# A new written order for the attention chunks and the shared groups, and the routed groups' targets read on ScalarE's queue

## The chip, the cores and the metric

One core of one Trainium2 chip runs the whole program: TensorE (PE, with its weight loads as PEld), VectorE (DVE), ScalarE (ACT), GpSimd (POOL), SyncE (SP, which here only issues DMAs), and 16 DMA engines. The metric is the device time of one execution in microseconds. The kernel before has a median of 1469.2 us over 3 runs (1464.93 to 1469.47).

## The reference, cut to what matters

Two layers act on x of 4 x 1024 tokens by 256 features. Each adds a gated attention and a gated feed-forward part to x. The change lies in the first layer: 16-head attention of the tokens to 64 context keys, and a mixture of 16 experts with 4 per token beside one shared expert.

```python
x = x + tanh(g_xattn[0]) * L0_xattn(layernorm(x), ctx)       # 16 heads, 64 keys
x = x + tanh(g_ffn[0]) * L0_ffn(layernorm(x))
# L0_ffn, per token:
scores = sigmoid(xt @ gate_w.T); _, idx = top_k(scores + gate_b, 4)
w = take_along_axis(scores, idx); w = 2.5 * w / sum(w)
y = sum over the 4 chosen e of w[e] * (silu(gate_e(xt)) * up_e(xt)) @ w2_e.T
y = y + (silu(gate_s(xt)) * up_s(xt)) @ w2_s.T               # shared expert
# then the second layer: attention over context and tokens, a ternary-weight product
```

## The kernel before, in words

Each engine has one instruction stream, written by hand in the order in which it runs; semaphores join them. A wait on an engine holds everything behind it on that engine.

**Attention chunks.** The 4096 tokens are 8 chunks c of 512 (four tiles j of 128 tokens). For chunk c the streams do: layer norm statistics on DVE (`statistics(1, c)`, L834 to L844: bn_stats, bn_aggr, minus the mean into `nmu` at L843, variance into `ve` at L844); the power -0.5 and a product on POOL (`rstd_of`, L644 and L646); four normalisations on ACT (`normalised`, L721) into the one tile `xn`; transposes on PE into the banks x0, x1 (L1085), moved to SBUF by ACT (all moves are L726); the query products q0, q1 (L1096), moved too; per tile the scores (L1106 a mask term, L1109), the row maximum and the shift on DVE (`shift`, L860 and L862), exp on ACT (L736), the row sum and its reciprocal on DVE (`row_sum`, L868 and L871), the scaling on POOL (`normalise`, L652); eight pairs of transposes pt0 to pt7 (L1118); values oT0, oT1 (L1128); outputs o0, o1 (L1138); and DVE's addition to x (`add`, L877).

The routing of chunk c runs one chunk later, among the attention of c + 1: `statistics(2, c)`, `rstd_of`, `normalised` (L721 again), the high half of the row in fp16 on ACT (`rows_high`, L753) and the low half on DVE (`rows_low`, L883), transposes r0, r1, logits (L1148), tanh (L761), `choose` on DVE (L888 to L921), `targets` (L926 to L931), `ranks` on PE (L1157 to L1162), `slots` (L939 to L948, which reads the rank bank at L939), and 16 `send`s on POOL (L659), indirect DMAs that scatter the rows to per-expert lists in HBM (`expert_rows`). The dense rows go to HBM by SP (`store_dense`). Beside each chunk ACT and DVE also split the weights of two experts into high and low fp16 halves (`high`, L713 and L714; `low`, L849 and L851).

All PSUM products of this part go round a ring of four banks in the fixed order of the list `order`: product i may be written only when product i - 4 has been read by the engine that the list names for it ("act" or "dve").

**Groups.** When the last chunk is out of the ring, the shared expert runs over 16 groups of 256 tokens, then the routed experts over 79 groups of 256 rows. For group g SP issues a DMA transpose of the rows (`shared_rows`, L599; routed L624) into one of 4 buffers; PE does gate and up (`group_gate_up`, L1218, 12 matmuls); ACT silu (L810); DVE the product with up (L1028); ACT the high half (L815); DVE the low half (L1033); PE the down product (`group_down`, L1229, 6 matmuls); DVE adds a shared result to x (L1039) or copies a routed one to one of 6 buffers (`group_out`, L1047). PE is two groups ahead with gate and up (DEEP = 3). Before the routed groups can start, 16 tails of the lists have to be filled with spare rows (`fill_tail`, L557, 272 KB each; 5 by ACT, 11 by SP between its shared transposes), for which the counts of all chunks must be known (`tables`, L960 gives the first table, L976 the second), and all sends and fills must have landed.

For a routed group SP also reads the targets of its 256 rows (L630, 1 KB into `gidx`, 8 buffers, in SP's queue behind the group's transpose), and POOL scatters the result with two indirect DMAs (L703), which wait for `gidx` and for the copy; the copy waits until the scatter six groups before has landed (`s_back`). SP's reads wait for the landing eight groups before. The next stage starts when the last scatter has landed.

## Time and profile before

| what | value |
|---|---|
| median of 3 runs | 1469.2 us |
| the profiled execution | 1465.75 us, span 1464.0 us |
| busy: PE, DVE, ACT, POOL | 77%, 69%, 45%, 34% of the span |
| mean granted TensorE clock | 0.884 |
| attention chunks and routing | to about 389 us |
| shared groups and tails | to about 434 us |
| routed groups | to 670 us |

Times in the rows are in us from the start of the span. A busy share is a mean over stages with different limits, so the stage is read first (the windows), then the engine that is busy in it, and then what ends that engine's waits (the bracket at the end of a timeline's row: idle time before it, and who ended it).

### The profile page before, as it was taken

What the parts mean: (1) busy time and instruction counts of PE and PEld (TensorE: products, weight loads), DVE (VectorE), ACT (ScalarE), POOL (GpSimd) and SP (SyncE); (2) the same over time, 40 slices, a digit from 0 to 9 for tenths busy, and PEclk for the clock granted to TensorE, in tenths of its full rate; (3) what the DMA queues carried; (4) which work ended last, traced back from release to release, by engine and by line L of the source; (5) the groups of instructions that cost most, each with busy time, mean ns of one, the idle gap of its engine ahead of it and who ended that gap; (6) DMA issues with size and microseconds to landing.
All of it is one profiled execution on the core that took longest, in us unless ns stands there. A gap on an engine that the chain in (4) does not pass through costs nothing. (4 is left out here: it accounts for less than half of the span.)

```text
span 1464.0 us, 25236 instructions
## 1 busy us (share of the span) xinstructions
PE 1126.2 (77%) x8327; PEld 606.6 (41%) x8327; DVE 1007.6 (69%) x1863; ACT 664.6 (45%) x1401; POOL 503.9 (34%) x576
## 2 busy tenths in 40 slices
PE   3786777775487777781877589999999999988858
PEld 2343344434375666660444123333333333331646
DVE  3677887875564544444996778888888888860665
ACT  1454344453232322220333066777776777775430
POOL 1226655666716766673000611112111111111110
PEclk7898879877699999995889589999999999995989
DMA  6011222222888888874796411211112111100003
GB/s 194 22 36 59 73 93 82 86 94 75 235 198 170 172 167 181 172 154 183 228 286 213 132 41 49 68 41 40 40 41 62 56 40 40 41 2 0 1 1 115
DMA packets 203515, 145.81 MB, mean 100 GB/s; under 512 B 134392, under 2 KB 178427, under 8 KB 203402
## 3 DMA queue, kind: packets, MB, share of 16 engines
q1 hardware_dynamic: 180778, 102.76, 28.1%
q0 software_dynamic: 13728, 34.64, 7.0%
q10 hardware_dynamic: 8896, 6.90, 1.6%
q8 instruction: 71, 1.16, 0.3%
q14 instruction: 42, 0.34, 0.1%
HBM read 53.19 MB, written 69.75 MB: 84 GB/s over the span
## 5 line engine op out<-in xcount | busy, mean ns | idle before, releaser
L1788 DVE TENSOR_REDUCE small<-ps 128x2 f32<-128x960 f32 (+6 forms) x384 | 379.0, 1041 | 56.7 <-PE ps L1843 56.5
L1767 ACT ACTIVATE region<-ps 128x512 f32<-128x512 f32 (+5 forms) x768 | 343.1, 533 | 107.9 <-PE ps L1857 106.5
L1738 POOL TENSOR_SCALAR_AFFINE_SELECT region<-region 128x512 f32<-128x512 f32 (+2 forms) x160 | 87.3, 546 | 425.7 <-ACT region L1767 425.7
L1857 PE MATMUL ps<-region 50*128 50x512 f16 (+5 forms) x896 | 197.7, 330 | 27.2 <-ACT region L1767 23.9
L1933 PE MATMUL ps<-region 128*32 128x512 f32 (+5 forms) x1792 | 191.6, 501 | 2.5 <-POOL region L1738 1.9
L703 POOL DMA_INDIRECT result_rows<-region,small x158 | 157.9, 999 | 99.2 <-DVE region L1047 58.4
L1218 PE MATMUL ps<-region 128*128 128x256 f16 x1140 | 149.8, 285 | 53.8 <-DMA region<-expert_rows 45.8
L1843 PE MATMUL ps<-region 48*128 48x480 f16 (+6 forms) x896 | 141.6, 334 | 13.5 <-DVE small L1788 11.3
L1218 PEld LDWEIGHTS ps<-region 128*128 (+1 forms) x1140 | 110.0, 102 | 88.9 <-issue 67.5
L1857 PEld LDWEIGHTS ps<-region 50*128 50x128 f16 (+1 forms) x896 | 54.4, 95 | 209.7 <-ACT region L1767 195.1
L1028 DVE SCALAR_TENSOR_TENSOR region<-ps,region 128x256 f32<-128x256 f32 x95 | 40.3, 424 | 128.9 <-ACT region L810 123.6
L652 POOL TENSOR_TENSOR region<-region,small 128x1024 f32<-128x1024 f32 x32 | 61.5, 1933 | 111.0 <-DVE small L871 110.9
L810 ACT ACTIVATE region<-ps 128x256 f32<-128x256 f32 x95 | 36.3, 383 | 133.6 <-PE ps L1218 129.3
L1229 PE MATMUL ps<-region 128*128 (+1 forms) x570 | 81.2, 281 | 9.0 <-DVE region L1033 9.0
L1838 PE MATMUL ps<-small 64*128 64x128 bf16 (+1 forms) x768 | 68.7, 245 | 16.7 <-POOL small L1719 11.6
L726 ACT ACTIVATE small<-ps 128x512 f32<-128x512 f32 x64 | 36.2, 590 | 88.8 <-PE ps L1096 53.4
L659 POOL DMA_INDIRECT expert_rows<-region,small x64 | 65.4, 1022 | 28.0 <-issue 17.1
L1529 PE MATMUL ps<-region 128*128 128x512 f16 (+1 forms) x240 | 56.1, 402 | 23.7 <-DVE region L1472 23.7
L659 POOL DMA_INDIRECT expert_rows<-rows_odd,small x64 | 64.7, 1012 | 23.2 <-issue 19.3
L1843 PEld LDWEIGHTS ps<-region 48*128 48x128 f16 x896 | 49.1, 97 | 51.3 <-DVE small L1788 47.2
L721 ACT ACTIVATE xn<-x_sb,small,rstd 128x256 f32<-128x256 f32 x64 | 33.1, 589 | 82.0 <-POOL small L646 82.0
L1096 PE MATMUL ps<-small 128*128 128x512 f32 x64 | 47.9, 918 | 27.2 <-DVE x_sb L877 19.3
(219 smaller groups left out, 1735.3 us busy)
## 6 DMA issues: line engine op xcount, KB each, us to landing
region<-result_rows SPq DMA_DIRECT2D x16, 1024.0 KB, 6.8
region<-v_parts SPq DMA_DIRECT2D x16, 576.0 KB, 4.0
v_parts<-region SPq DMA_DIRECT2D x14, 576.0 KB, 6.9
region<-k_parts SPq DMA_DIRECT2D x96, 68.0 KB, 2.2
region<-q_parts SPq DMA_DIRECT2D x96, 64.0 KB, 2.1
k_parts<-region SPq DMA_DIRECT2D x16, 272.0 KB, 4.4
x_sb<-in_x ACTq DMA_DIRECT2D x8, 512.0 KB, 9.0
region<-in_w13T SPq DMA_DIRECT2D x16, 256.0 KB, 3.2
```

Source lines behind the costliest of these rows:

```text
L652: nc.gpsimd.tensor_tensor(pr, pr, rsum[:, j, :].unsqueeze(2).to_broadcast([P, H, CTX]), ALU.mult).then_inc(s_prob, 1)
L659: nc.gpsimd.indirect_dma_start(out=xs, out_offset=bass.IndirectOffsetOnAxis(ap=sloti[:, b, at_:at_ + 1], axis=0), in_=rows[b][:, at_ // TO ...
L703: nc.gpsimd.indirect_dma_start(out=ys, out_offset=bass.IndirectOffsetOnAxis(ap=gidx[:, r % I_BUFS, j:j + 1], axis=0), in_=y_out[:, r % Y_B ...
L1218: ins = nc.tensor.matmul(ps[:, 2 * (g % DEEP) + half_, 0:GROUP], w, xgT[:, g % G_BUFS, part, kh, :], start=n == 0, stop=n == 5)
L1229: ins = nc.tensor.matmul(ps[:, 6 + g % 2, j * D:(j + 1) * D], (hgh, hgl)[part][:, g % DEEP, j * P:(j + 1) * P], flat((w2h, w2l)[low][:, ba ...
L1738: nc.gpsimd.affine_select(out=t, in_=t, compare_op=ALU.is_ge, fill=0.0, base=r0, pattern=[[0, G], [1, w]], channel_multiplier=-1).then_inc ...
L1767: nc.scalar.activation(dst, src, ACT.Exp, scale=SCALE).then_inc(s_exp, 1)
L1788: nc.vector.tensor_reduce(nmp[:, qt, :, p0:p0 + np_, place], s_pair(n + first)[:, :, 0:np_ * nk] .rearrange("p e (h k) -> p e h k", h=np_) ...
L1838: nc.tensor.matmul(o, mask_id[rows[half], part, :], mask_dg[rows[half], part, 0:np_, :], start=part == 0, stop=False, skip_group_check=True)
L1843: ins = nc.tensor.matmul(banks[half][:, p * nk:(p + 1) * nk], q_of(r, v)[:, p0 + p, qt * P:(qt + 1) * P], k_of(r, v)[:, p0 + p, k0:k0 + nk ...
L1857: ins = nc.tensor.matmul(o, k_of(rr, tbuf)[:, pair, kt * P:kt * P + rows], q_of(rr, tbuf)[:, pair, q0:q0 + nq], start=True, stop=True)
L1933: ins = nc.tensor.matmul(ps[32 * h:32 * h + 32, O_BANK, q0 - hf * CH:q0 - hf * CH + nq], vg[0:rows, buf, (kt * G + h) * 32:(kt * G + h + 1 ...
```

## The change

It has four parts.

1. The written order of the attention chunks. The transposes and moves of x (`inputs`) become ring entries of their own, done for chunk c + 2 at the end of chunk c. ACT does the experts' high halves ahead of the query moves. DVE does `statistics(1, c + 2)` right behind `statistics(2, c - 1)`, and `add(c)` ahead of row sums 2 and 3. PE does `ranks(c - 1)` behind the last scores. POOL sends 4 rows of the newest chunk late in a chunk and the other 12 at the front of the next.
2. Two sets of `nmu`, `nmr`, variance and rstd in place of one, so that waits on them look one event further back.
3. The first shared groups are written among the routing of the last chunk. Gate and up of a group share one bank, shared results have one bank (`DEEP`), so the groups need only four banks while the ring still runs. ACT fills 8 tails among groups 6 to 13, SP the other 8.
4. The reads of the routed groups' targets go from SP's queue to ACT's (`load_targets`), three groups ahead, between a group's silu and its high half. Each now loads the group's start from the table again.

```diff
-            order = queries(0)
+            order = inputs(0) + queries(0) + inputs(1)
             for c in range(CHUNKS):
-                order += queries(c + 1) if c < LAST else []
+                order += queries(c + 1)
                 order += probs_of(c, range(2)) + rows_of(c - 1) + probs_of(c, range(2, 4)) + logits_of(c - 1)
-                order += probs_of(c, range(4, 8)) + ranks_of(c - 1) + outputs_of(c)
+                order += probs_of(c, range(4, 8)) + values_of(c)
+                if c < LAST:
+                    order += ranks_of(c - 1) + inputs(c + 2) + outputs_of(c)
+                else:
+                    order += outputs_of(c) + ranks_of(c - 1)
...
+            def load_targets(eng, r):
+                if r >= I_BUFS:
+                    old = r - I_BUFS
+                    eng.wait_ge(s_back[old % Y_BUFS], (old // Y_BUFS + 1) * GT * 16)
+                first = start(eng, FIRSTS + r)
+                eng.dma_start(gidx[:, r % I_BUFS, :],
+                              xs[bass.ds(first, GROUP), bass.ds(first >> SHIFT, 1)].bitcast(I32)
+                              .rearrange("(j p) n -> p (j n)", p=P),
+                              allow_slow_non_contiguous=True).then_inc(s_idx[r % I_BUFS], 16)
...
@@ POOL, chunk c; EARLY, LATE = 4, 6 @@
                     if c >= 2:
-                        send(c - 2, 8, 16)
+                        send(c - 2, EARLY, LATE)
+                    if c + 2 < CHUNKS:
+                        rstd_of(1, c + 2)
+                    if c >= 2:
+                        send(c - 2, LATE, 16)
                     if c < LAST:
                         normalise(c + 1, range(2))
-                    if c and c < LAST:
-                        send(c - 1, 0, 2)
-                    if c + 2 < CHUNKS:
-                        rstd_of(1, c + 2)
-                    if c and c < LAST:
-                        send(c - 1, 2, 8)
-                    if c < LAST:
+                        if c:
+                            send(c - 1, 0, EARLY)
                         normalise(c + 1, range(2, TC))
...
@@ ACT, chunk c @@
+                    for expert in experts_beside(c):
+                        high(*expert)
                     if c < LAST:
                         move_queries(c + 1)
                     if c:
                         normalised(2, c - 1)
-                    for expert in experts_beside(c):
-                        high(*expert)
...
                     silu(g)
+                    if FIRSTS <= g < ALL_GROUPS - AHEAD:
+                        load_targets(act, g - FIRSTS + AHEAD)
+                    hidden_high(g)
...
@@ DVE, chunk c @@
+                        second(c - 1)
+                    if c + 2 < CHUNKS:
+                        statistics(1, c + 2)
                     for expert in experts_beside(c):
                         low(*expert)
...
-                    if c + 2 < CHUNKS:
-                        statistics(1, c + 2)
-                    if more:
-                        shift(c + 1, 3)
-                        row_sum(c + 1, 2)
-                        row_sum(c + 1, 3)
+                    shift(c + 1, 3)
                     add(c)
+                    row_sum(c + 1, 2)
+                    row_sum(c + 1, 3)
...
@@ PE, chunk c @@
-                    if c:
-                        ranks(c - 1)
                     values(c)
                     if more:
                         scores(c + 1, 3)
+                        if c:
+                            ranks(c - 1)
+                    if c + 2 < CHUNKS:
+                        inputs_of(c + 2)
                     outputs(c)
...
@@ PE, after the chunks @@
+                group_step(0)
+                transposed(LAST, 2, ("r0", "r1"))
+                group_step(1)
+                logits(LAST)
+                group_step(2)
+                ranks(LAST)
```

## Rows read from the trace of the kernel before

**Rows 1.** Busy by stage: us, PE, PEld, DVE, ACT, POOL (instructions), PEclk, DMA share, GB/s.
```profile
223.39:265.10 41.71, 29.01 (x138) 17.43 (x136) 33.75 (x74) 19.09 (x36) 26.25 (x24) 0.88 0.25 85
341.20:370.10 28.90, 19.14 (x91) 14.37 (x91) 11.42 (x40) 11.38 (x22) 18.23 (x20) 0.65 0.33 98
389.20:429.50 40.30, 28.88 (x228) 23.25 (x225) 24.14 (x50) 11.84 (x28) 15.80 (x16) 0.84 0.99 245
442.20:669.80 227.60, 168.14 (x1373) 132.16 (x1370) 106.97 (x232) 62.55 (x154) 157.91 (x158) 0.94 0.81 162
```

**Rows 2.** DVE's timeline in one chunk: start, us, instruction, count [idle before <- releaser].
```profile
245.55 2.15 DVE L943 TENSOR_TENSOR small<-small 128x256 f32<-128x256 f32 x1
...
255.40 1.22 DVE L868 TENSOR_REDUCE small<-region 128x16 f32<-128x1024 f32 x1 [2.67 <-ACT region L736]
...
261.40 2.19 DVE L843 TENSOR_SCALAR small<-mv 128x4 f32<-128x4 f32 x1
...
268.03 0.69 DVE L849 SCALAR_TENSOR_TENSOR region<-region 128x512 f16<-128x512 f32 x1 [4.37 <-ACT region L714]
```

**Rows 3.** ACT's timeline in the same chunk, the normalisation of layer 1.
```profile
252.35 2.08 ACT L721 ACTIVATE xn<-x_sb,small,rstd 128x256 f32<-128x256 f32 x4 [9.57 <-POOL small L646]
```

**Rows 4.** PE's timeline in the same chunk.
```profile
253.09 2.71 PE L1085 MATMUL ps<-ident,xn 128*128 128x128 f32 x8 [5.28 <-ACT xn L721]
258.90 5.33 PE L1096 MATMUL ps<-small 128*128 128x512 f32 x8 [3.10 <-DVE x_sb L877]
...
267.10 1.04 PE L1085 MATMUL ps<-ident,xn 128*128 128x128 f32 x8
```

**Rows 5.** POOL's timeline in the same chunk, and before the last.
```profile
245.51 1.90 POOL L652 TENSOR_TENSOR region<-region,small 128x1024 f32<-128x1024 f32 x1 [7.84 <-DVE small L871]
...
259.79 3.76 POOL L652 TENSOR_TENSOR region<-region,small 128x1024 f32<-128x1024 f32 x2
263.74 1.04 POOL L644 TENSOR_TENSOR rstd<-ve,half 128x4 f32<-128x4 f32 x1 [0.19 <-DVE ve L844]
...
270.79 0.96 POOL L659 DMA_INDIRECT expert_rows<-rows_odd,small  x1 [0.30 <-issue]
...
342.95 3.76 POOL L652 TENSOR_TENSOR region<-region,small 128x1024 f32<-128x1024 f32 x2
```

**Rows 6.** SP's routed transposes and target reads by source: ns min/median/max, first and last start.
```profile
L624 SPq DMA_TRANSPOSE region<-expert_rows x79: 1234/1257/2087, 429.6 to 652.2; - x79
...
L630 SPq DMA_DIRECT2D small<-expert_rows x79: 381/386/1676, 431.1 to 653.7; - x79
```

**Rows 7.** POOL's scatters of results by source.
```profile
L703 POOL DMA_INDIRECT result_rows<-region,small x158: 982/985/2137, 442.2 to 667.7; - x158
```

**Rows 8.** Waits between engines, 442 to 670 us: total us, times, longest us.
```profile
POOL result_rows L703 <- DVE region L1047: 58.4, 33, 30.6
```

**Rows 9.** Busy while PE's first transposes of the chunk run (columns of rows 1).
```profile
253.10:255.80 2.70, 2.67 (x8) 1.43 (x8) 0.40 (x1) 2.70 (x5) 2.09 (x3) 0.50 0.32 103
```

**Rows 10.** DVE's timeline: ends of statistics (chunks 0, 5, 6), last addition, first table.
```profile
92.97 0.16 DVE L844 TENSOR_SCALAR ve<-mv 128x4 f32<-128x4 f32 x1
...
305.23 0.16 DVE L844 TENSOR_SCALAR ve<-mv 128x4 f32<-128x4 f32 x1
...
341.15 0.16 DVE L844 TENSOR_SCALAR ve<-mv 128x4 f32<-128x4 f32 x1
...
369.36 0.75 DVE L877 SCALAR_TENSOR_TENSOR x_sb<-ps,tg,x_sb 128x512 f32<-128x512 f32 x1 [0.97 <-PE ps L1138]
...
388.88 0.28 DVE L960 TENSOR_TENSOR small<-ps,small 1x16 int32<-1x16 f32 x1
```

**Rows 11.** ACT's queue: its five tail fills, in one stretch.
```profile
390.18 8.20 ACTq L557 DMA_DIRECT2D expert_rows<-region  x5
```

**Rows 12.** ACT's loads of a table word for the fills, by source: ns min/median/max.
```profile
L556 ACTq TENSOR_LOAD <-small x5: 467/690/1132, 389.3 to 396.3; - x5
```

**Rows 13.** The sends to the lists, from issue to landing, 180 to 420 us.
```profile
DMA to landing us min/median/max: 2.4/2.5/6.0
```

More of the change, by code:

```diff
@@ L405, in flamingo @@
         junk = view(small, "junk", [P, 4], F32)
-        nmu = view(small, "nmu", [P, TC], F32)
-        nmr = view(small, "nmr", [P, TC], F32)
+        nmu = view(small, "nmu", [P, 2, TC], F32)
+        nmr = view(small, "nmr", [P, 2, TC], F32)
+        vars_ = view(small, "vars", [P, 2, TC], F32)
+        rstds = view(small, "rstds", [P, 2, TC], F32)
         gw_sb = view(small, "gw", [P, KH, E], F32)
@@ L1053, in _, with group_step @@
-                for g in range(ALL_GROUPS):
+                    shift(c + 1, 3)
+                    add(c)
+                    row_sum(c + 1, 2)
+                    row_sum(c + 1, 3)
+                add(LAST)
+                second(LAST)
+                targets(LAST - 1)
+                slots(LAST - 1)
+                def group_step(g):
                     if g + DEEP - 1 < ALL_GROUPS:
@@ L1061, in _ @@
                         group_hidden_low(g + DEEP - 1)
+                for g in range(DEEP - 1):
+                    group_hidden(g)
+                    group_hidden_low(g)
+                rows_low(LAST)
+                group_step(0)
+                group_step(1)
+                choose(LAST)
+                targets(LAST)
+                slots(LAST)
+                tables()
+                for g in range(2, ALL_GROUPS):
+                    group_step(g)
                     if g == SPLIT_AT:
@@ new lines, in group_down @@
+                def group_down(g, e):
+                    eng.wait_ge(s_ghl, g + 1)
+                    if 0 < g < FIRSTS:
+                        eng.wait_ge(s_yout, g)
+                    elif g >= FIRSTS + 2:
+                        eng.wait_ge(s_yout, g - 1)
+                    elif g >= FIRSTS:
+                        eng.wait_ge(s_act, moved(turn[LAST, "lg"]))
+                        eng.wait_ge(s_dve, moved(turn[LAST, "count"]))
+                    for j in range(GT):
+                        for n, (part, low) in enumerate(three):
+                            ins = nc.tensor.matmul(result(g)[:, j * D:(j + 1) * D],
+                                                   (hgh, hgl)[part][:, g % DEEP, j * P:(j + 1) * P],
+                                                   flat((w2h, w2l)[low][:, bass.ds(e, 1), :]), start=n == 0, stop=n == 2)
+                    ins.then_inc(s_gy, 1)
@@ L1165, in _, with expert, inputs_of @@
+                def expert(g):
+                    return start(eng, g) >> SHIFT if g >= FIRSTS else E
+                def inputs_of(c):
+                    transposed(c, 1, ("x0", "x1"))
+                inputs_of(0)
                 queries_of(0)
                 wait_moved(0, "q1")
-                for j in range(TC):
-                    scores(0, j)
+                scores(0, 0)
+                scores(0, 1)
+                inputs_of(1)
+                scores(0, 2)
+                scores(0, 3)
@@ L1223, in group_down @@
-                def group_down(g, e):
-                    eng.wait_ge(s_ghl, g + 1)
-                    if g >= 2:
-                        eng.wait_ge(s_yout, g - 1)
-                    for j in range(GT):
-                        for n, (part, low) in enumerate(three):
-                            ins = nc.tensor.matmul(ps[:, 6 + g % 2, j * D:(j + 1) * D],
-                                                   (hgh, hgl)[part][:, g % DEEP, j * P:(j + 1) * P],
-                                                   flat((w2h, w2l)[low][:, bass.ds(e, 1), :]), start=n == 0, stop=n == 2)
-                    ins.then_inc(s_gy, 1)
@@ L1234, in expert, with group_step @@
-                def expert(g):
-                    return start(eng, g) >> SHIFT if g >= FIRSTS else E
-                experts = []
-                for g in range(DEEP - 1):
-                    experts.append(expert(g))
-                    group_gate_up(g, experts[-1])
-                for g in range(ALL_GROUPS):
+                ranks(LAST - 1)
+                def group_step(g):
                     if g + DEEP - 1 < ALL_GROUPS:
@@ L1247, in _ @@
                     group_down(g, experts.pop(0))
+                experts = []
+                for g in range(DEEP - 1):
+                    experts.append(expert(g))
+                    group_gate_up(g, experts[-1])
+                group_step(0)
+                transposed(LAST, 2, ("r0", "r1"))
+                group_step(1)
+                logits(LAST)
+                group_step(2)
+                ranks(LAST)
+                wait_free(LAST, "count")
+                nc.tensor.matmul(slot(LAST, "count")[:, 0:E], onesb[:], counts[:, CHUNKS, :], start=True,
+                                 stop=True).then_inc(s_full, 1)
+                for g in range(3, ALL_GROUPS):
+                    group_step(g)
         reset(region1, region2, small)
```

222 lines of the change are left out of this document (116 added, 106 removed).

## The prediction

> **What bounds the kernel now.** I read the table by stages first [rows 1]. The change touches the first 670 us, and four stretches of it behave differently. In the attention chunks (the first row is one chunk of about 42 us) DVE is busy 33.75 of 41.71 us and no DMA or PE share is near full. Round the last chunk, 341 to 370 us, every engine is idle a third of the time or more. From 389 to 430 us the 16 DMA engines are busy 0.99. In the routed groups (442 to 670) the DMA share is 0.81 and POOL, whose 157.9 us of issues leave out the 0.30 us between two of them, is the fullest engine.
>
> Second view, the timelines of one chunk. DVE's instructions follow each other without a gap but for two waits [rows 2]: 2.67 us before the third row sum (for ScalarE's exp) and 4.37 us before the low halves of the experts' weights (for ScalarE's high halves). ScalarE is late for both because of what stands ahead in its queue: it sat 9.57 us for POOL's rstd of chunk c+2, whose statistics DVE makes late in the chunk [rows 3], and the high halves (L713, L714) stand behind the query moves, which wait for PE, which waited 3.10 us for DVE's addition [rows 4]. So add, queries, query moves, normalise, high halves, low halves, scores is a loop round four engines, and it closes once a chunk. Two DVE instructions are long only because POOL's multiplication L652 runs beside them [rows 2, 5]: L943 takes 2.15 us and ends when L652 does, L843 takes 2.19 and ends when L652 does.
>
> Third, the routed groups. SP issues 79 transposes from 429.6 to 652.2, 222.6/78 = 2.854 us apart, and between two of them stands one read of targets of 0.39 us [rows 6]. POOL's 158 scatters start from 442.2 to 667.7 [rows 7], and of the 58.4 us that it stood for DVE's results 30.6 lie before the first [rows 8]: 27.8 us inside the stage.
>
> **The change part by part.**
>
> *Attention order.* The x transposes of chunk c+2 now run at the end of chunk c, so the queries no longer wait for the addition; the bank of q0 and q1 is freed by ScalarE's x moves. High halves go ahead of the query moves: 4.37 us gone. statistics(1, c+2) moves to the front of the chunk, POOL's rstd right behind it, ScalarE has it some 10 us before it needs it: 2.67 gone. The two sets of nmu, rstd and nmr let both rstd stand at once and cost no instruction. Left on DVE, with the small gaps between its instructions: 41.71 - 4.37 - 2.67 = 34.67 us. The addition now stands before row sums 2 and 3, so POOL's two L652 end only some 0.6 us after DVE reaches L843, where they now hold it 2.0: 34.67 - 1.5 = 33.2.
>
> What is late next: POOL. Its queue per chunk is 16 sends of 0.96 + 0.30, four L652 of 1.9 and two rstd of about 1.4, together 20.2 + 7.6 + 2.8 = 30.6 us; the sends 4 to 16 of c-2 now fill the 7.84 us in which it waited for a row sum [rows 5]. Walking through one chunk, POOL's last L652 ends 0.1 us before DVE's statistics end, so the two are level. PE has its queries done early and then waits some 4 us for that last L652. In the trace 5.28 us of waiting were followed by a granted clock of 0.50 (1.2 GHz) [rows 9]; its 8 transposes then took 2.71 us, and 1.04 in the dense stretch at 267 [rows 4]. I charge the first scores at half clock to DVE: 1.3 us. Chunk: 34.5 us. Ends: 30.9 (no L652 in DVE's way: 34.67 - 2.0 - 1.7) and 39.2 (POOL's 31.4 with hiccups plus the 7.84 us wait unfilled).
>
> From the end of the statistics of chunk 0 to those of chunk 5 the trace has 305.23 - 92.97 = 212.3 us [rows 10]; five of 34.5 are 172.5: -39.8. Chunk 6, which has no further chunk to prepare, 341.15 - 305.23 = 35.9, becomes 34.5 - 2.1 (no statistics) = 32.4: -3.5. In the start the low halves wait no longer for the query moves, but inputs(1) come ahead of scores: -2 (0 to -4). Sum -45.3.
>
> *Last chunk.* Now POOL's rstd of chunk 6 stands behind two L652 that end at 346.7 [rows 5], 5.4 us after the statistics (341.3), and from there to the end of the last addition (370.1 [rows 10]) it is 23.4 us. Afterwards those L652 are done when the statistics are, and the same chain starts 5.4 us earlier: -5.4.
>
> *Shared groups beside the last routing.* DVE reaches the tail table (L960) 18.8 us after the last addition [rows 10]. In the new order statistics (2.2), targets and slots of chunk 6 (2.5), two shared groups of hidden halves (2.8), the wait for ScalarE's normalise and rows_high (3.1), rows_low and two group steps (5), and choose to slots (8, partly a wait for the logits) stand ahead: 24 to 25 us, so +6. After it come 16 tail fills, 16 sends and the transposes: 40.3 us at 0.99 busy [rows 1], so DMA and not compute is the limit. Two transposes have gone ahead; a routed group's whole DMA is 0.81 x 227.6/79 = 2.3 us [rows 1], its transpose the larger part, so I take 3.3 us for two, and the gate comes some 37 us after the tail table. The hidden shared groups therefore buy little. Sum +2; ends -12 (fills overlapping better, tail table no later) and +10 (tail table 6 later, three more ScalarE table loads, and ScalarE's eight fills, about 1.64 us each by the five that took 8.20 [rows 11], standing ahead of silu).
>
> *Targets on ScalarE.* SP loses 0.39 + 0.27 us a group and then paces at about 2.1. POOL's two scatters are 2 x (0.99 + 0.30) = 2.58 us [rows 5, 7] and become the pace. ScalarE gains a load of a start-table word (0.47 to 1.13 us in its fills, while DMA was full [rows 12]), register work of some 0.4, and the issue of 0.39: 1.3 to 1.5 us between silu (0.38) and the high half (0.42), about 2.2 us a group, under 2.58. DEEP groups in flight hide the longer path: a group's hidden half is wanted two groups later. From 2.87 a group (225.5/78.5 [rows 7]) to 2.68 (POOL's 2.58, hiccups, late landings): 79 x 0.19 = -15. Ends: -22 (all at 2.6) and +5.
>
> The Trainium skill ("DMA: Bandwidth & Descriptors", section "Issuing engines are not separate DMA queues") says that DMAs of all issuing engines share the same 16 engines and that issuing from several saves only the sequencer's time. By it SP's 0.66 us x 79 = 52 us is the most that the move can free, and none of it if the 16 engines set the pace. The trace has them at 0.81, or 184 us of 227.6; that is rival 1.
>
> **Sum**, against the profiled execution's 1465.75 us (span 1464.0): -45.3 - 5.4 + 2 - 15 = -63.7, so 1402. The median of the runs, 1469.2, is 3.4 above that execution; I give 1403.
>
> **Rivals.**
> 1. *The routed stage gains nothing*: the DMA engines, or ScalarE waiting for landings, hold it at 2.87. For: mean share 0.81 hides stretches at full. Against: POOL stood 27.8 us for DVE only, and 184 us is under 204. Time 1403 + 15 = 1418.
> 2. *POOL paces the attention* at 39.2: five chunks x 4.7 = +23.5, 1426. For: 30.6 of 33.2 us leaves little room for a long send. Against: its waits are at the places that the sends now fill. With rival 1: 1441.
> 3. *The new order does nothing for DVE*: PE's outputs(c) now wait for slots(c-1) through the bank ring (o1 after rank), and what DVE won it waits for the addition. Then only the queue move counts, 1450; with rival 1 about 1465. Against: slots read the rank 5 us before the addition is due and PE's second half of outputs takes 1.8.
> 4. *Slower*: ScalarE's read for group r+3 waits for the landing of scatter r-5, and high halves of r and silu of r+1 queue behind it, DVE behind those. The loop over four groups is 1.29 + landing + 4.3 us (read 1.4, high half and silu 0.9, hidden 0.5, result 0.7, POOL's 0.8). With landings of 2.5, the nearest row's median, it gives 2.0 us a group, with its maximum of 6.0 [rows 13] 2.9. To eat the 48.7 us of the other terms the pace must be 2.87 + 0.62 = 3.49, landings of 8.4 us on the mean; at 9.5 the pace is 3.77 and the time 1403 + 86 = 1489.
>
> **How the numbers follow.** Forecast 0.52 (its own range 1388 to 1417), rival 1 0.19, rival 2 0.12, both 0.06, rival 3 0.06, of which 0.02 near 1465, rival 4 0.05. Range 1384 (chunk 33.2 and routed -21, with -5 at the tail) to 1440, which leaves out rivals 3 and 4 and some of the fastest. About 0.3% (4.4 us) is what a measurement here can tell from no change: faster 0.93, same 0.02, slower 0.05.
>
> **What would show it.** Right: DVE's waits for L713/L714's results and for the third exp gone; statistics(2, c) 33 to 36 us apart; L843 under 1 us; the first routed transpose near 380; POOL's scatters 2.6 to 2.75 apart with hardly a wait for the result copies. Wrong: POOL without an idle stretch and chunks at 38 or more; PE waiting before L1138's second bank; the tail fills ending before 370; ScalarE idle before its high half for a DMA of result rows; transposes landing later than the groups need them.

## The result, and the profile after

The changed kernel takes 1411.07 us (median of 4 runs, 1404.78 to 1412.54) against 1468.1 us for the kernel before (4 runs): a ratio of 0.9606, 95% interval 0.9573 to 0.9640. Its profiled execution takes 1411.37 us (span 1409.6). The forecast was 1403, with 1384 to 1440 around it.

The stages first, as in [rows 1]. Each chunk runs from one `statistics(2, c)` to the next; the last four stretches run to the last addition, to the tail table, to the first routed transpose, and from the first routed result to the last scatter. The gate is what the first routed transpose waits for: all sends to the lists and all tail fills must have landed.

```profile
core 0: us, PE busy (x) PEld busy (x) DVE busy (x) ACT busy (x) POOL busy (x), PEclk, DMA share, GB/s
90.53:125.01 34.48, 27.35 (x134) 16.44 (x134) 32.57 (x75) 18.84 (x34) 14.84 (x12) 0.91 0.17 56
125.01:161.25 36.24, 29.10 (x134) 18.06 (x134) 33.90 (x76) 18.96 (x34) 26.28 (x24) 0.88 0.29 98
161.25:198.10 36.85, 29.75 (x134) 18.06 (x134) 33.85 (x75) 18.95 (x34) 26.89 (x24) 0.87 0.27 97
198.10:231.63 33.53, 27.08 (x134) 16.63 (x134) 31.88 (x76) 18.83 (x34) 26.81 (x24) 0.91 0.31 106
231.63:265.48 33.85, 27.38 (x134) 16.77 (x134) 31.90 (x75) 18.84 (x34) 27.12 (x24) 0.90 0.30 105
265.48:301.46 35.98, 23.14 (x118) 14.68 (x118) 31.96 (x65) 15.17 (x26) 25.96 (x22) 0.78 0.29 99
301.46:323.40 21.94, 19.10 (x90) 14.50 (x90) 8.87 (x31) 11.03 (x19) 13.85 (x16) 0.64 0.46 119
323.40:345.45 22.05, 15.65 (x120) 12.03 (x120) 16.23 (x60) 7.48 (x17) 14.87 (x15) 0.92 0.75 213
345.45:388.51 43.06, 24.75 (x165) 18.45 (x166) 21.25 (x44) 7.56 (x20) 19.60 (x20) 0.72 0.95 230
400.02:611.77 211.75, 170.10 (x1380) 129.27 (x1380) 109.17 (x235) 56.78 (x155) 157.67 (x158) 0.96 0.88 173
```

The chunk of 41.7 us in [rows 1] has become 33.5 to 36.9 us with DVE busy 31.9 to 33.9 of it. The routed stretch has lost 15 us at the same POOL time, and its DMA share has risen from 0.81 to 0.88.

DVE in chunk 5, then in chunk 6 (start, duration, engine, line, operation; the bracket is the idle time ahead):

```profile
236.26 1.22 DVE L911 TENSOR_REDUCE small<-ps 128x16 f32<-128x1024 f32 x1 [0.77 <-PE ps L1171]
240.15 1.23 DVE L911 TENSOR_REDUCE small<-ps 128x16 f32<-128x1024 f32 x1 [0.28 <-PE ps L1171]
249.47 0.22 DVE L982 SCALAR_TENSOR_TENSOR region<-small 128x64 int32<-128x64 f32 x1
253.61 2.15 DVE L994 TENSOR_TENSOR small<-small 128x256 f32<-128x256 f32 x1
264.61 0.80 DVE L894 TENSOR_SCALAR small<-mv 128x4 f32<-128x4 f32 x1
...
270.25 1.23 DVE L911 TENSOR_REDUCE small<-ps 128x16 f32<-128x1024 f32 x1 [2.90 <-PE ps L1171]
283.46 2.21 DVE L982 SCALAR_TENSOR_TENSOR rows_odd<-small 128x64 int32<-128x64 f32 x1
289.59 2.15 DVE L994 TENSOR_TENSOR small<-small 128x256 f32<-128x256 f32 x1
```

Both waits of [rows 2], for the third exp and for the high halves, are gone; what is left are short waits for the scores. Three instructions are long, L894, L982 and L994, and POOL's queue shows why: each ends with one of its multiplications or up to 0.3 us after it.

```profile
253.58 1.90 POOL L675 TENSOR_TENSOR region<-region,small 128x1024 f32<-128x1024 f32 x1 [0.72 <-DVE small L922]
261.63 3.76 POOL L675 TENSOR_TENSOR region<-region,small 128x1024 f32<-128x1024 f32 x2
283.67 1.91 POOL L675 TENSOR_TENSOR region<-region,small 128x1024 f32<-128x1024 f32 x1
289.56 1.90 POOL L675 TENSOR_TENSOR region<-region,small 128x1024 f32<-128x1024 f32 x1 [3.98 <-DVE small L922]
```

In the routed groups POOL's waits for DVE (total, times, longest) can be held against [rows 8]: there 58.4 with 30.6 before the first scatter, 27.8 inside; here 12.0 inside, of which 23 of the 28 waits are the ordinary 0.30 us between two scatters. The scatters run from 401.6 to 611.8, 2.68 us a group. The third row, of what waited for their landing, is rival 4's wait: ScalarE stands 55.5 us in 17 places behind its read. It costs little, but not nothing: the five real waits of POOL, 0.73 to 1.27 us and 5.0 together, each follow one of these places. The last three rows are one of them, where ScalarE's 5.20 us (a DMA's landing, so the bracket names no engine) reach POOL as 0.86.

```profile
POOL result_rows L725 <- DVE region L1061: 40.8, 29, 28.8
...
L725 POOL DMA_INDIRECT result_rows<-region,small x158: 984/986/1781, 401.6 to 611.8; - x158
  ACT region L798: 55.5, 17
...
469.66 0.42 ACT L798 ACTIVATE region<-region 128x256 f16<-128x256 f32 x1 [5.20 <-issue]
470.11 0.43 DVE L1047 TENSOR_TENSOR region<-region 128x256 f16<-128x256 f32 x1 [4.53 <-ACT region L798]
472.30 0.98 POOL L725 DMA_INDIRECT result_rows<-region,small  x1 [0.86 <-DVE region L1061]
```

### The profile page after: what moved, and what is told of

The parts are those of the page before. It is cut to its first block and busy times, and to the rows that moved or that the text cites. A ratio compares the mean times of both kernels' runs of the same rounds, so it can differ in the third digit from the quotient of the medians.

```text
span 1409.6 us, 25476 instructions
## 1 busy us (share of the span) xinstructions
PE 1113.5 (79%) x8327; PEld 599.3 (43%) x8327; DVE 1006.2 (71%) x1863; ACT 657.6 (47%) x1401; POOL 509.4 (36%) x576
## 3 DMA queue, kind: packets, MB, share of 16 engines
q8 instruction: 71, 1.16, 0.3%
## 5 line engine op out<-in xcount | busy, mean ns | idle before, releaser
L1868 DVE TENSOR_REDUCE small<-ps 128x2 f32<-128x960 f32 (+6 forms) x384 | 378.9, 1040 | 56.8 <-PE ps L1923 56.5
L725 POOL DMA_INDIRECT result_rows<-region,small x158 | 158.6, 1004 | 81.3 <-DVE region L1061 40.8
L798 ACT ACTIVATE region<-region 128x256 f16<-128x256 f32 x95 | 39.6, 416 | 162.0 <-DVE region L1042 62.6
L1256 PE MATMUL ps<-region 128*128 (+1 forms) x570 | 81.6, 282 | 31.9 <-DVE region L1047 17.2
L1047 DVE TENSOR_TENSOR region<-region 128x256 f16<-128x256 f32 x95 | 40.2, 423 | 85.2 <-ACT region L798 83.5
L1180 PE MATMUL ps<-ident,region 128*128 128x128 f32 x256 | 43.9, 316 | 46.6 <-POOL region L675 45.0
L1256 PEld LDWEIGHTS ps<-region 128*128 128x128 f16 x570 | 55.0, 101 | 47.1 <-issue 37.6
L1171 PE MATMUL ps<-region,small 128*128 128x512 f32 x128 | 74.0, 663 | 0.0
L760 ACT ACTIVATE region<-region 128x1024 f32<-128x1024 f32 x32 | 33.9, 1058 | 81.6 <-DVE region L913 81.6
```

What stands on the lines that cost most here:

```text
L725: nc.gpsimd.indirect_dma_start(out=ys, out_offset=bass.IndirectOffsetOnAxis(ap=gidx[:, r % I_BUFS, j:j + 1], axis=0), in_=y_out[:, r % Y_B ...
L1171: ins = nc.tensor.matmul(o, qT[:, m, j * P:(j + 1) * P], kbd[:, m, c // 2, :], start=False, stop=True)
L1256: ins = nc.tensor.matmul(result(g)[:, j * D:(j + 1) * D], (hgh, hgl)[part][:, g % DEEP, j * P:(j + 1) * P], flat((w2h, w2l)[low][:, bass.d ...
L1868: nc.vector.tensor_reduce(nmp[:, qt, :, p0:p0 + np_, place], s_pair(n + first)[:, :, 0:np_ * nk] .rearrange("p e (h k) -> p e h k", h=np_) ...
```

## The experiments

Times are medians, beside runs of the kernel before on the same chip (1464.5 to 1467.1 us); the changed kernel itself (1411.1) was not run again beside them. Chunk times and waits are those of one profiled execution of each kernel.

**1. The order alone.** The reads go back behind SP's transposes.

```diff
                     sp.dma_start_transpose(... xs[bass.ds(first, GROUP), E:ROW] ...)
+                    read_targets(sp, g - FIRSTS, first)
...
-                        for r in range(AHEAD):
-                            load_targets(act, r)
...
-                    if FIRSTS <= g < ALL_GROUPS - AHEAD:
-                        load_targets(act, g - FIRSTS + AHEAD)
```

> The new order with the reads of the targets back on SP, one behind each transpose. Theory (SP's queue set the routed pace before, and the move alone changed it): the scatters fall back from 2.68 to 2.85-2.88 us a group, the first scatter to the last takes 225 us rather than 210, SP hardly waits for the gate products, the stages before the first routed transpose keep their times within 1 us, and the time is 1411 + 15 = 1426. Rival (the routed pace came with the new order: other banks, silu and high half split on ScalarE): 2.68 stays and the time is 1411.

1424.0 us, ratio 0.9712 (0.9677 to 0.9747); 2.855 us a group. One part of the theory fails: with the same code ahead of it, the first routed transpose stands 61.0 us behind the last addition and not 65.1. That stretch varies from one execution to the next, which matters for the tail below.

**2. The reads alone**, in the old order:

```diff
-                    sp.dma_start(gidx[:, r % I_BUFS, :], ...)
...
                     silu(g)
+                    if FIRSTS <= g < ALL_GROUPS - 3:
+                        load_targets(g - FIRSTS + 3)
+                    hidden_high(g)
```

> The old order with only the reads of the targets moved to ScalarE's queue, three groups ahead, between silu and the high half. Theory (the two parts of the change are independent and add): the routed pace goes from 2.87 to 2.68, every stage before it keeps its time, 1468 - 15 = 1453. Rival (the move needs the new order's free ScalarE or its banks): the pace stays at 2.8 or more and the time at 1463 to 1470.

1451.8 us, ratio 0.9897 (0.9875 to 0.9920); 2.69 us a group. The routed stretches of the two, from first result to last scatter:

```profile
395.45:621.07 225.62, 166.14 (x1380) 128.88 (x1380) 107.73 (x235) 62.98 (x155) 156.34 (x157) 0.98 0.81 164
```

```profile
440.13:652.90 212.77, 169.74 (x1380) 126.96 (x1377) 108.94 (x235) 56.34 (x155) 156.76 (x157) 0.97 0.85 172
```

42.1 us for the order and 14.4 for the reads are 56.5, and both together gave 57.0: within the intervals (some 5 and 3 us) the two parts add. Both rivals of experiments 1 and 2 fall, and rival 1 of the prediction with them.

**3. Statistics late.** `statistics(1, c + 2)` and its rstd on POOL go back to their old places, the rest of the new order stays. DVE's part:

```diff
-                    if c + 2 < CHUNKS:
-                        statistics(1, c + 2)
                     for expert in experts_beside(c):
                         low(*expert)
...
                         slots(c - 1)
+                    if c + 2 < CHUNKS:
+                        statistics(1, c + 2)
```

> The changed kernel with statistics(1, c+2) put back on DVE behind slots, and POOL's rstd of it behind the first two multiplications; the rest of the new order stays. Theory (ScalarE's wait for the rstd, 9.57 us in the old chunk, comes back and with it DVE's wait for the third exp, 2.67 us; and the 2.0 us of statistics no longer fill DVE's wait for the first scores): 2.7 + 1 to 2 us in five chunks, 1411 + 21 = 1432. Rival (the rstd is early enough in either place, because the inputs' transposes were moved to the end of the chunk): the chunks keep their times within 0.5 us, 1411 +- 3.

1458.4 us, ratio 0.9953 (0.9929 to 0.9976): 47 us worse than the changed kernel, twice the theory's 21. The old wait did not come back where it was. One chunk of 44.4 us:

```profile
206.40 2.15 DVE L994 TENSOR_TENSOR small<-small 128x256 f32<-128x256 f32 x1
219.88 0.75 DVE L928 SCALAR_TENSOR_TENSOR x_sb<-ps,tg,x_sb 128x512 f32<-128x512 f32 x1 [6.28 <-PE ps L1200]
213.45 2.98 PE L1148 MATMUL ps<-ident,xn 128*128 128x128 f32 x8 [12.38 <-ACT xn L743]
216.22 5.39 PE L1200 MATMUL ps<-small 128*128 128x256 f32 x16
212.70 2.08 ACT L743 ACTIVATE xn<-x_sb,small 128x256 f32<-128x256 f32 x4 [15.95 <-POOL small L669]
```

The inputs' transposes of c + 2 (L1148) now stand ahead of the outputs (L1200) on PE. With the rstd late ScalarE waits 15.95 us, PE 12.38, the outputs and DVE's addition 6.28. Without the early statistics the transposes of the inputs hold up everything behind them there.

**4. High halves behind.**

```diff
-                    for expert in experts_beside(c):
-                        high(*expert)
                     if c < LAST:
                         move_queries(c + 1)
                     if c:
                         normalised(2, c - 1)
+                    for expert in experts_beside(c):
+                        high(*expert)
```

> The changed kernel with ScalarE's high halves put back behind the query moves and the second norm; the rest of the new order stays. Theory (the queries no longer wait for the addition, but the second norm waits for POOL, which has its last multiplications ahead of it: ScalarE's high halves end 4 to 5 us later, DVE's low halves stand before the first shift and come 2.3 to 3.2 us late): 2.7 us in each of six chunks, 1411 + 16 = 1427. Rival 1 (the prediction's own price, the 4.37 us wait of the old chunk, returns whole): 1411 + 26 = 1437. Rival 2 (with the queries early, the place of the high halves is of no account): 1411.

1419.3 us, ratio 0.9689 (0.9645 to 0.9733). The middle chunks take 37.3 us. The theory's place is right, its price half: DVE waits 2.37 us for the high halves, but the scores are there when it is done, so the old wait of [0.77] for them goes.

```profile
204.06 0.69 DVE L900 SCALAR_TENSOR_TENSOR region<-region 128x512 f16<-128x512 f32 x1 [2.37 <-ACT region L736]
205.94 1.22 DVE L911 TENSOR_REDUCE small<-ps 128x16 f32<-128x1024 f32 x1
```

**5. Scores first.** On PE the first scores go ahead of the transposed probabilities, into the gap in which it waits for POOL.

```diff
-                    transposed_probs(c, range(2))
                     if more:
                         wait_moved(c + 1, "q1")
                         scores(c + 1, 0)
+                    transposed_probs(c, range(2))
```

> On PE the first scores of chunk c+1 ahead of the first two pairs of transposed probabilities of chunk c, and not behind them. PE then makes them while POOL still multiplies. Theory (DVE bounds the chunk, and its waits for the scores, 0.5 to 2.9 us for the first and 0.3 to 0.5 for the second, 9.5 us over six chunks, lie on the path): the waits go, the chunks take 33.4 us on the mean and not 35.0, 1411 - 9.5 = 1401.5. Rival (POOL's queue, sixteen sends of 1.27, four multiplications and two rstd, 31 of 34 us, bounds the chunk too): DVE waits for the transposed probabilities' followers instead, the chunks lose 0.3 us, 1409.

1398.9 us, ratio 0.9524 (0.9489 to 0.9559), a little more than the theory gave. Chunks 2 to 5 take 32.7 us each with DVE busy 31.8, chunk 1 35.0 and chunk 6 37.6. Chunks 4 and 5, where L982 was not held before, lose 0.9 and 1.2 us, about their old waits for the scores (0.75 and 1.05). Chunks 2 and 3 lose 3.6 and 4.2: their waits (1.44 and 2.10) and the 2.0 us of L982, which no longer meets a multiplication. In chunk 6 nothing is won: DVE waits 1.72 us for ScalarE and 3.16 for the second scores, and L961 is held 2.14 us.

```profile
221.60:254.30 32.70, 27.37 (x139) 16.36 (x138) 31.80 (x75) 18.74 (x34) 26.15 (x24) 0.99 0.31 109
254.30:291.90 37.60, 23.03 (x112) 14.55 (x113) 31.89 (x65) 15.06 (x26) 24.84 (x22) 0.76 0.28 95
```

**6. Slots late.** On DVE the writing instruction of targets and all of slots but the read of the rank bank go behind `shift(c + 1, 3)`, out of the way of POOL's second multiplication.

```diff
                     if c:
-                        slots(c - 1)
+                        place_of(c - 1)
                     shift(c + 1, 3)
+                    if c:
+                        slots(c - 1)
...
```

> On DVE the last of targets (L982) and all of slots but its read of the rank bank go behind shift(c+1, 3), where POOL's second multiplication has ended; the order on PE is that of the changed kernel. Theory (DVE instructions that read and write SBUF are held while POOL multiplies: L994 took 2.15 us beside L675 and 0.43 without, L982 2.2 and 0.22; but the chunk is closed by the scores behind POOL's last multiplication, so DVE wins the time and waits it out): L994 falls to 0.43 and L982 to 0.22, the chunks with the held L982 (36.2, 36.9, 36.0 us) come to some 34, the others lose 0.5 at most: 1411 - 8 = 1403. Rival 1 (DVE's queue alone bounds the chunk): 1.7 us in each of six chunks and 2.0 in three of them, 1411 - 16 = 1395. Rival 2 (POOL, whose four sends now start as late as before, bounds it): 1409 to 1412.

1400.4 us, ratio 0.9557 (0.9517 to 0.9597): all chunks at 34.2 to 35.0, none at 36. Chunks 2, 3 and 6, the ones with the held L982, lose 1.8 to 2.6 us, the others grow by 0.3 to 0.7. That is 4.7 us in all; the median's 10.6 are not the hold alone. In the profiled execution (1398.1) another 4.0 us lie between the last chunk and the last addition, in code that the edit does not touch and at a granted clock of 0.82 (the last row; the changed kernel took 21.94 us there at 0.64). The held instructions are short now (L992 is the old L982, L997 the old L994), but another one, L894, stands 3.12 us and ends with POOL's last pair of multiplications (224.76 + 3.76). A hold that is taken off one instruction fell on the next.

```profile
218.43 0.22 DVE L992 SCALAR_TENSOR_TENSOR rows_odd<-small 128x64 int32<-128x64 f32 x1
218.56 0.42 DVE L997 TENSOR_TENSOR small<-small 128x256 f32<-128x256 f32 x1
225.44 3.12 DVE L894 TENSOR_SCALAR small<-mv 128x4 f32<-128x4 f32 x1
224.76 3.76 POOL L675 TENSOR_TENSOR region<-region,small 128x1024 f32<-128x1024 f32 x2
...
296.96:314.95 17.99, 15.68 (x98) 11.78 (x99) 8.92 (x31) 10.69 (x19) 13.91 (x16) 0.82 0.58 129
```

**7. Scores first and slots late together.**

> The first scores ahead of the transposed probabilities (which took the time to 1398.9 and five chunks to 32.7 us, DVE busy 31.8 of them) and the slots behind shift(c+1, 3) together. Theory (with the scores ready in time DVE's queue is the bound, and the 1.7 us in which L994 is held by POOL's multiplication come off it whole until POOL's 31.0 us are reached): 31.1 us a chunk, 1398.9 - 1.6 x 6 = 1389. Rival (POOL is the bound at 32.7 already, since its last four sends start only when the slots are there): the chunks stay at 32.4 or more, 1397 to 1400.

1408.4 us, ratio 0.9626 (0.9561 to 0.9692), with single runs from 1402.5 to 1419.6: worse than experiment 5, and no better than 6. L894 is held 3.11 us, and chunks 2 to 4 take 34.1 to 34.7 as in experiment 6. Chunks 5 and 6 take 38.3 and 38.1. There POOL's first multiplication meets other instructions of `choose`, L966 (0.17 us alone) and L961 (0.42), and POOL then stands 5.56 and 6.57 us for the next row sum. So the theory falls, and the rival too: POOL is not the bound in these two chunks, which are 4 us slower than in experiment 6; the hold has moved once more.

```profile
244.59 2.57 DVE L966 TENSOR_TENSOR small<-small 128x16 bf16<-128x16 bf16 x1
281.69 2.78 DVE L961 TENSOR_TENSOR small<-small 128x256 f32<-128x256 f32 x1
...
252.69 1.90 POOL L675 TENSOR_TENSOR region<-region,small 128x1024 f32<-128x1024 f32 x1 [5.56 <-DVE small L922]
290.75 1.90 POOL L675 TENSOR_TENSOR region<-region,small 128x1024 f32<-128x1024 f32 x1 [6.57 <-DVE small L922]
```

**8. Fewer sends ahead of the last multiplications** (slots late kept).

```diff
-                EARLY, LATE = 4, 6
+                EARLY, LATE = 2, 4
```

> The late slots, and on POOL two sends of the newest rows ahead of the last two multiplications of a chunk and not four (EARLY 2, LATE 4); PE's order is that of the changed kernel. Theory (with the late slots alone the hold only changed its victim: L994 fell to 0.43 us, but POOL's last two multiplications then started 1.2 us after the row sums allow, and L894, which stood beside them, was held 3.12 us; two sends fewer, 2.5 us, let them start earlier): L894 near 0.9, 34.2 us a chunk become 32.3, where POOL's own 27.0 of work, 4.8 between sends and 0.3 beside them are the bound, 1400.4 - 6 x 1.9 = 1389. Rival (the sends taken from there stand ahead of the first two multiplications in the next chunk, which come 2.5 us later, and the probabilities' transposes with them): 34 us or more a chunk, 1398 to 1403.

1391.0 us, ratio 0.9476 (0.9441 to 0.9510), the fastest measured, and the theory's mechanism: L894 is at 0.80, and the five chunks take 32.9 us on the mean. From chunk 2 on POOL has no idle stretch but one of 1.4 to 1.7 us for the slots (and up to 0.3 between two instructions), while DVE waits 0.6 to 1.7 us for the first scores.

```profile
215.80 3.75 POOL L675 TENSOR_TENSOR region<-region,small 128x1024 f32<-128x1024 f32 x2 [0.26 <-DVE small L922]
```

```profile
218.78 0.80 DVE L894 TENSOR_SCALAR small<-mv 128x4 f32<-128x4 f32 x1
```

**9. Experiments 5, 6 and 8 together.**

> The first scores ahead of the transposed probabilities, the late slots, and EARLY 2, LATE 4. Theory (DVE then waits for no scores and is held by no multiplication but 0.9 us at L894, so that POOL's queue, some 32 us, is the bound): 32.0 us a chunk, against 32.7 with the scores alone, 1398.9 - 0.7 x 6 - 2 (chunk 6) = 1393. Rival (POOL without idle time closes the chunk through its last multiplications whatever DVE wins, as with scores and slots together, 34.2 to 38.3 us): 1400 or more.

1395.1 us, ratio 0.9527 (0.9502 to 0.9552). The five chunks take 33.1 us: on top of experiment 8 the scores' place is worth nothing. The theory's 1393 is 2 us off, but its premise does not hold: DVE now waits 1.2 to 3.3 us a chunk for the second scores. POOL waits up to 0.6 us for row sums in chunks 2 to 5, so it is the bound, or nearly.

**10. Tail fills denser.** ScalarE's eight fills two to a shared group.

```diff
-                    if TAILS_FROM <= g < TAILS_FROM + ACT_TAILS:
-                        fill_tail(act, g - TAILS_FROM)
+                    if TAILS_FROM <= g < TAILS_FROM + ACT_TAILS // 2:
+                        fill_tail(act, 2 * (g - TAILS_FROM))
+                        fill_tail(act, 2 * (g - TAILS_FROM) + 1)
```

> ScalarE's eight tail fills two to a shared group (groups 6 to 9) and not one to each of 6 to 13; nothing else. Theory (the gate before the routed groups is held by the last fill, which stands in ScalarE's queue behind the silu of shared group 12, and that waits for a late transpose; SP waited 5.61 us for it): the last fill is issued near 372 and not at 385.2, the first routed transpose leaves near 383 and not at 388.5, 1411 - 5.5 = 1405.5. Rival (the 16 DMA engines, 0.95 busy between the tail table and the gate, set it): the gate moves by less than 1 us, 1411. Second rival: two fills ahead of a silu hold shared groups 6 to 9 back by 1.6 us each, gate/up of group 12 is what SP then waits for, and the time is 1411 to 1416.

1411.7 us, ratio 0.9624 (0.9598 to 0.9650): no gain. ScalarE's last fill left at 367.9 and not at 385.2, but SP's transposes were then held in their issue, and its own last fill went out at 377.4. In SP's queue of this kernel, against the 1.23 us of a routed one:

```profile
364.13 5.64 SPq L628 DMA_TRANSPOSE region<-dense_rows  x1
371.25 5.33 SPq L628 DMA_TRANSPOSE region<-dense_rows  x1
384.80 1.23 SPq L655 DMA_TRANSPOSE region<-expert_rows  x1
```

The gate moved by 2.3 us against the tail table (40.8 and not 43.1 us behind it), and the first routed result came 4.5 us later behind it. The time is the rival's. That the DMA engines set the gate is not shown by it: in the runs that leave this stretch as it is, the gate stands 38.5 to 43.1 us behind the table, and 40.8 lies among them.

**11. Last routing ahead of all shared groups**, as before the change. DVE's part of the edit (ScalarE and PE likewise):

```diff
-                for g in range(DEEP - 1):
-                    group_hidden(g)
-                    group_hidden_low(g)
                 rows_low(LAST)
-                group_step(0)
-                group_step(1)
                 choose(LAST)
...
```

> The changed kernel with the last chunk's routing put back ahead of all shared groups on ScalarE, DVE and PE; the rest of the new order, the eight tail fills on ScalarE and the reads of the targets too, stays. Theory (shared groups between the steps of the last routing buy nothing, since the DMA engines are what the gate waits for, and they push the tail table back): the tail table comes 19 us after the last addition and not 22.05, the first routed transpose 59 to 60 us after it and not 60.9 to 65.1, and the time is 1411 - 3 = 1408. Rival (the shared groups that now run ahead are what lets the first routed group start 11.5 us behind its gate): the gate is 3 us earlier, the first result 3 to 8 us later, 1411 to 1416.

1413.1 us, ratio 0.9648 (0.9616 to 0.9680). The tail table comes at 18.9 us, as the theory says, but the gate only 49.1 behind it, 68.0 after the last addition and not 59 to 60. The theory falls, and so does the rival, whose gate was to be earlier. With the shared groups ahead the gate stands 60.7 to 65.1 us behind the last addition, so they do save something, 2.9 us or more in this one profile, which the medians hardly show.

**12. Chunk 6's sends ahead of the last additions**, on top of experiment 8. DVE's and POOL's parts (PE's ranks and the bank order follow):

```diff
+                targets(LAST - 1)
+                place_of(LAST - 1)
+                slots(LAST - 1)
                 add(LAST)
                 second(LAST)
-                targets(LAST - 1)
-                place_of(LAST - 1)
-                slots(LAST - 1)
...
+                send(LAST - 1, 0, 4)
                 rstd_of(2, LAST)
-                send(LAST - 1, 0, 16)
+                send(LAST - 1, 4, 16)
```

> The kernel with the late slots and EARLY 2, and in the last chunk the rank, targets and slots of chunk 6 ahead of the last additions (DVE waited 4.0 us there), with four of its sends ahead of the last rstd; everything else as in e10_slots_early2. Theory (the gate before the routed groups follows POOL's last sends: 32 of them, 41 us, are left at the last addition, and in the changed kernel none of chunk 6's can start before the last statistics, where the kernel before had its slots ready): chunk 6's sends start 6 to 8 us earlier, chunk 7's 16 start when their slots are there and not behind them, the last send leaves 4 us earlier against the last addition (44.5 and not 48.4 us after it), the first routed transpose 60.5 and not 65.1, and the time is 1391 - 4.5 = 1386.5. Rival (the 16 DMA engines, 0.95 busy from the tail table to the gate, set it, or the shared groups do): the last send moves and the gate does not, 1390 to 1392.

1391.9 us, ratio 0.9482 (0.9457 to 0.9506), no change from experiment 8. The last send left 42.6 us after the last addition and not 48.4, the first transpose 61.9 and not 65.1. SP then waited 6.7 us for landings where it had waited 4.6. The last send moved as the theory says. Whether the gate followed cannot be told: 61.9 lies within the 60.7 to 65.1 that the unchanged tail gives from run to run, and the time is the rival's.

```profile
SPq L648 <- DMA expert_rows<-region: 6.7, 1, 6.7
```

## Why the prediction was right, and where its sizes were off

| term | forecast | measured | from, to |
|---|---|---|---|
| start | -2 | -2.6 | 93.1, 90.5 |
| five chunks | -39.8 | -37.3 | 212.3, 174.95 |
| chunk 6 | -3.5 | +0.1 | 35.9, 36.0 |
| last chunk to last addition | -5.4 | -6.9 | 28.8, 21.9 |
| to the tail table | +6 | +3.3 | 18.8, 22.05 |
| to the first routed transpose | -4 | +2.4 | 40.7, 43.1 |
| routed groups to the last scatter | -15 | -14.9 | 238.1, 223.3 |
| after it | 0 | +1.5 | 798.1, 799.6 |
| sum | -63.7 | -54.4 | 1465.75, 1411.37 |

The forecast lies 8 us from the median, and the mechanism is the one forecast in the two terms that carry it, the five chunks and the routed groups. Two tail terms cancel in part (2.7 us better, 6.4 worse), which is luck. The 1403 itself carries only 1 of the 3.4 us between that execution and the median, without a reason.

**Attention: right, mis-sized by 6 us.** The two waits went as said. The first scores after PE's wait were charged at 1.3 us; chunks 1 to 5 show 0.5 to 1.7 and 0.3 to 0.5 us, 1.27 on the mean. What was missed is the hold by POOL. The prediction saw it at L843 and L943 [rows 2, 5], took 1.5 off at the first and kept the second: L894 is 0.80, L994 still 2.15. It did not see that L982, 0.22 us, could fall into a multiplication too. In chunks 2, 3 and 6 it does (2.2 us each), and these are the three chunks of 36 and more. That is 4.0 of the five chunks' 174.95. In chunk 6 it is 2.0 more, and the wait for the scores, 2.90 + 0.28 where 1.3 was charged, another 1.9, together about the 3.6 that the term lacks. Experiment 6 shows the hold in these three chunks, experiment 5 the wait on the path in chunks 4 and 5; in chunk 6 it did not take the wait away. The term behind, to the last addition, goes with the granted clock: the same code took 18.0 and 18.3 us in experiments 6 and 7 at 0.82 and 0.79, and 21.9 here at 0.64.

**POOL was level with DVE, as stated**, and closer than its chance as a rival: experiment 8 shows it closing the chunks at 32.4 to 33.4 us once DVE is faster. Rival 3's wait is there, and with it one of the prediction's signs of being wrong, PE waiting before the second bank of the outputs: 9.3 us in five of the six chunks, 3.0 at most (waits between 90 and 302 us).

```profile
PE ps L1200 <- DVE small L990: 9.3, 5, 3.0
```

It costs no time in the chunk: DVE's addition (L928) follows without idle time in all six, and PE then still waits for POOL's last multiplications (3.62 us in chunk 5). The rival falls by that, and not by the wait's absence.

**Price by part was wrong inside the right sum.** The statistics' place was priced at 2.67 us a chunk and the high halves' at 4.37, old waits read from [rows 2], some 13 and 22 us over five chunks. Undone one at a time in the new order they cost 47 us and 8 us in all. An old wait tells what the whole new order may win, not what each edit wins: the edits lean on each other.

**Tail: the step that failed.** The forecast was +2 for the stretch from the last addition to the first routed transpose; it went from 59.5 to 65.1, +5.6. With chunk 6's term this puts the first routed transpose at 388.5 and not near 380. What is steady in it is the tail table, 21.8 to 23.1 us behind the last addition in the runs with this order (experiments 11 and 12 change it) and 18.8 before. "The gate comes some 37 us after the tail table", 4 us less than before, failed: it counted two transposes off a stretch at 0.99 busy, and this code's 38.5 to 43.1 us lie round the old 40.7. In all it gave 61.0 us in experiment 1 and 60.7 to 65.1 in the others.

What sets the gate stays open. The prediction overlooked that POOL's sends now come later: 32 of them are left at the last addition and start 4.9 us after it, where before chunk 6's stood at 365.9, 4.2 us ahead of it. But the last send leaves 16.7 us ahead of the gate and the last fill, ScalarE's, 3.3 us ahead of it, and that fill stands behind a silu for which ScalarE waited 6.65 us for PE. Experiment 12 moved the last send by 5.8 us and the gate by 3.2, no more than the spread; experiment 10 moved ScalarE's fills and won nothing; experiment 11 shows that the interleaving is not what makes the gate late.

```profile
L682 POOL DMA_INDIRECT expert_rows<-rows_odd,small x64: 957/963/1864, 152.5 to 371.8; - x64
L586 ACTq DMA_DIRECT2D expert_rows<-region x8: 548/549/699, 355.6 to 385.2; - x8
```

**Routed groups: right.** 2.68 forecast, 2.678 measured, and experiment 2 gives -14.4 with this part alone. POOL's two scatters are the floor: from one group to the next 2.58 us in 7 of 10 cases. The 0.10 us over it was an allowance, not worked out; that it fits so closely is luck. The rule of the Trainium skill weighed in the prediction ("DMA: Bandwidth & Descriptors", section "Issuing engines are not separate DMA queues") agrees with the trace: the 16 engines move the same data, their share rises from 0.81 to 0.88, and only issue time was saved. It counted because SP's issue set the pace before: afterwards SP waits 37.0 us for PE in this stage, where it had waited 1.2.

## What to carry to other kernels

Where two engines are level, look at both: a hold that is removed from one instruction comes back at the next one that meets the other engine (experiments 6 and 7), until the other engine's work is moved as well (experiment 8). When a product is moved ahead of another in an in-order queue, what feeds it must be moved first: the same transposes win with an early rstd and lose nearly everything with a late one (experiment 3). Price a reordering by the chunk's new closing loop, not by adding up the old waits.

## What the hardware showed

While POOL multiplies (reading SBUF), DVE instructions with two SBUF inputs, and the small tensor_scalar, are held to its end: L994 2.15 us against 0.43, L966 2.57 against 0.17 (experiment 7), L894 up to 3.46 against 0.17 (experiment 6). Reductions and instructions with a PSUM input beside it are not (L919 1.16 to 1.21 and L913 1.22 to 1.23, with and without). The Trainium skill ("SBUF — State Buffer", section "Who interferes with whom") names the same pairs as contending and says that the one that issues first holds the ports for its whole instruction. On which instructions are held the traces agree. On the order the rows agree only in part: L942, which starts in the same 0.01 us as a multiplication, is not held (0.23, and the multiplication takes 1.99 and not 1.90), but L982 starts 0.2 us and L966 0.6 us ahead of the multiplication with which they end.

A DMA transpose took 1.23 us to issue on SP in the routed groups, and up to 5.64 us where the DMA engines were full (experiment 10, share 1.00 from 344 to 385 us).

With the first scores in PE's gap (experiment 5) the granted clock of chunks 2 to 5 rose: it was between 0.87 and 0.91 and came to between 0.92 and 0.99. The chunks at 0.92 and at 0.99 take the same 32.7 us, so within these bounds the clock did not set their length.
